# Projection order of a batch's prologue, and written step orders for its attention groups

## The chip, the cores and the metric

One core of one Trainium2 chip runs the whole kernel in one launch. The metric is device time in microseconds (us). The kernel before took 3039.46 us, the median of three runs (3035.17 to 3039.74).

The core's engines are TensorE (PE: matrix products; PEld: its weight loads), VectorE (DVE), ScalarE (ACT), GpSimd (POOL) and SyncE (SP), whose queue starts all DMA transfers here. Each runs its own instruction stream in order; they wait for each other on semaphores.

## The reference, cut to what matters

Two transformer layers on x of shape (2, 1024, 1024), float32. The change concerns the attention of both:

```python
x = x + _L0_attn_ref(_layernorm(x), wq, wk, wv, wo)      # 32 heads of 32, 8 key/value heads
x = x + _L0_ffn_ref(_layernorm(x), ...)                   # mixing of four streams
x = x + _L1_attn_ref(_layernorm(x), Wq, Wk, Wv, Wo)       # the same shape, other rotation
x = x + _L1_ffn_ref(_layernorm(x), ...)                   # gated experts
# attention, per batch entry and head:
q, k, v = x @ wq, x @ wk, x @ wv          # q and k are rotated
scores = q k^T / sqrt(32), causal mask
out = softmax(scores) v;  out @ wo
```

## The kernel before, in words

`attention` (one call per layer, prefix `a_` in the trace) works through two batch entries of 1024 rows. Heads come in eight groups of four, which share one key/value head. A batch has these stages:

- **Prologue.** Six projections of 128 columns each, a *p* in the code, in two halves *c* of 512 rows: keys, keys, queries of group 0, values, values, queries of group 1. Each half is eight pieces of three products (high and low parts of a split float32). VectorE takes a half out of PSUM and rotates it (lines 686, 687), GpSimd finishes the rotation (462, 464), ScalarE and GpSimd split it in two parts (590, 470), SP stores it to DRAM (335, 342) and loads it back stacked in the layout of the scores (352 keys, 345 queries). Values are transposed (953). From the fifth projection on, the row scores of group 0 are interleaved: a *row-score step* S is one bank of query x key products (839), whose maximum VectorE takes (698, 701). 38 such steps give the row maxima of a group; MT transposes them (848), and SP carries them by DRAM into the queries' last row (358, 360).
- **Groups 0 to 5**, the steady ones, as a loop over pairs, three passes. A group's own work is 12 units ST:e.h (four heads, one product each, 886, with ScalarE's exponential, 605, and GpSimd's mask on the diagonal, 494), the products with the values V (902) and with ones D (915), sums of two units on GpSimd (509) and the normalisation of two query halves, NORM (VectorE 746 to 752, behind ScalarE's copies 612 and 618). Interleaved are the row scores S of the next group and the queries' projection P of the group after the next.
- **Group 6** has no projection, **group 7** no row scores. In the first batch group 7 also brings in the next batch's rows: load XL (399), statistics XS (661), scale XN (670), transpose XT (830), evacuation and split XC (584, 677), and the first half of the next batch's first projection.

In every stage the order of instructions is that of a list of steps. For the steady groups it is the text `ORDER`, parsed once; groups 6 and 7 take the same list with what they lack left out, and the next batch's steps are put into it by rules (`iteration`). `bank_plan` gives each S, P, MT and VT step a PSUM bank: in the prologue two of them for S and four for projections, in the groups three for both. In the prologue S follows every piece of 19 (`S_STEPS`), two at a time.

## Time and profile before

| | us |
|---|---|
| median of three runs | 3039.46 |
| the profiled execution's own time | 3036.84 |
| its span in the trace | 3035.1 |
| prologue, batch 0 and 1 of the first layer | 98.0, 91.9 |
| first group, the same | 61.6, 59.5 |
| a steady group | 46.7 |
| last group, batch 0 and 1 | 68.3, 35.4 |

A stage is cut at the first ST product of a group. The trace gives for each instruction its start from the span's beginning, its length and the idle time of its engine before it. Products on PE overlap, so their lengths sum to more than the time; the distance of two starts is what one costs. PEclk is the granted clock of TensorE, 1.00 at full speed.

### The profile page before, as it was taken

What the parts mean: (1) busy time and instruction counts of PE and PEld (TensorE: products, weight loads), DVE (VectorE), ACT (ScalarE), POOL (GpSimd) and SP (SyncE); (2) the same over time, 40 slices, a digit from 0 to 9 for tenths busy, and PEclk for the clock granted to TensorE, in tenths of its full rate; (3) what the DMA queues carried; (4) which work ended last, traced back from release to release, by engine and by line L of the source; (5) the groups of instructions that cost most, each with busy time, mean ns of one, the idle gap of its engine ahead of it and who ended that gap; (6) DMA issues with size and microseconds to landing.
All of it is one profiled execution on the core that took longest, in us unless ns stands there. A gap on an engine that the chain in (4) does not pass through costs nothing. (4 is left out here: it accounts for less than half of the span.)

```text
span 3035.1 us, 50649 instructions
## 1 busy us (share of the span) xinstructions
PE 2620.5 (86%) x15056; PEld 1810.9 (60%) x15056; DVE 1819.1 (60%) x4485; ACT 1081.8 (36%) x2317; POOL 1123.2 (37%) x801
## 2 busy tenths in 40 slices
PE   7799997889998799653768999988799996996999
PEld 6556653655654588542645555545556553885887
DVE  5577775547776433688764666764577774225453
ACT  2155454135555211352511445552155454002000
POOL 7265653445664100000043555636265552001111
PEclk9999998999999899766979999989899998998999
DMA  4223221323231421000233323222323223433111
GB/s 149 87 81 104 64 75 63 117 71 104 77 86 42 161 69 55 0 0 7 83 132 95 106 61 93 73 83 74 90 81 103 64 75 112 146 131 146 63 69 42
DMA packets 121079, 252.95 MB, mean 83 GB/s; under 512 B 12720, under 2 KB 39728, under 8 KB 120880
## 3 DMA queue, kind: packets, MB, share of 16 engines
q1 hardware_dynamic: 120912, 251.03, 25.9%
q8 instruction: 67, 1.10, 0.2%
q14 instruction: 100, 0.82, 0.1%
HBM read 166.57 MB, written 84.41 MB: 83 GB/s over the span
## 5 line engine op out<-in xcount | busy, mean ns | idle before, releaser
L605 ACT ACTIVATE a_prob<-a_pst 128x512 f32<-128x512 f32 (+3 forms) x1536 | 660.7, 493 | 581.8 <-PE a_pst L886 576.2
L698 DVE CUSTOM_DVE_ANT_0 a_psh<-a_psh,a_edge 128x128 f32<-128x128 f32 (+3 forms) x1024 | 479.5, 518 | 247.7 <-PE a_psh L839 218.8
L839 PE MATMUL a_psh<-a_kst,a_qst 127*128 127x512 f32 (+3 forms) x1536 | 494.6, 371 | 79.4 <-DMA a_qst<-q 52.7
L886 PE MATMUL a_pst<-a_qst,a_kst 128*128 128x512 f32 (+2 forms) x1536 | 490.1, 374 | 22.7 <-DMA a_qst<-rowmax 17.8
L509 POOL TENSOR_TENSOR a_prob<-a_prob 128x2048 f32<-128x2048 f32 (+1 forms) x96 | 405.6, 4226 | 241.6 <-PE a_ppv L902 241.6
L839 PEld LDWEIGHTS a_psh<-a_kst,a_qst 127*128 127x128 f32 x1536 | 272.1, 191 | 321.9 <-DVE a_mx L701 104.7
L701 DVE TENSOR_REDUCE a_mx<-a_psh 128x1 f32<-128x512 f32 x512 | 328.2, 685 | 117.3 <-PE a_psh L839 116.4
L886 PEld LDWEIGHTS a_pst<-a_qst,a_kst 128*128 128x128 f32 x1536 | 289.4, 195 | 164.2 <-ACT a_prob L605 105.0
L902 PE MATMUL a_ppv<-a_prob,a_vg 128*32 128x512 f32 (+3 forms) x3072 | 319.8, 503 | 0.0
L915 PE MATMUL a_pden<-a_prob,a_ones 128*32 128x512 f32 (+3 forms) x2304 | 220.4, 475 | 13.8 <-POOL a_prob L509 13.8
L494 POOL TENSOR_SCALAR_AFFINE_SELECT a_prob<-a_prob 128x512 f32<-128x512 f32 x256 | 162.4, 640 | 184.7 <-ACT a_prob L605 184.3
L818 PE MATMUL a_psh<-a_xT_hi,a_w_hi 128*128 128x512 f32 x512 | 210.7, 412 | 16.3 <-DVE a_swp L687 8.5
L818 PE MATMUL a_psh<-a_xT_hi,a_w_lo 128*128 128x512 f32 x512 | 205.1, 401 | 0.0
L818 PE MATMUL a_psh<-a_xT_lo,a_w_hi 128*128 128x512 f32 x512 | 204.8, 400 | 0.0
L462 POOL TENSOR_TENSOR a_swp<-a_swp,a_sin 128x512 f32<-128x512 f32 x80 | 103.4, 1293 | 269.4 <-DVE a_swp L687 258.2
L1480 PE MATMUL h_pout<-h_w,h_o 128*128 128x512 f32 x720 | 167.7, 392 | 0.3 <-DVE h_x L1357 0.3
L1480 PEld LDWEIGHTS h_pout<-h_w,h_o 128*128 128x128 f32 x720 | 134.0, 188 | 28.3 <-issue 0.7
L455 POOL TENSOR_TENSOR a_w_lo<-a_wraw,a_w_hi 128x1024 fp32r<-128x1024 f32 x50 | 119.0, 2381 | 74.4 <-ACT a_w_hi L578 59.5
L698 DVE DVE_READ_ACCUMULATOR2_ANT a_mx<- 128x1 f32 x1024 | 144.3, 141 | 2.9 <-issue 2.9
L902 PEld LDWEIGHTS a_ppv<-a_prob,a_vg 128*32 128x32 f32 x3072 | 70.2, 109 | 104.3 <-issue 64.8
L915 PEld LDWEIGHTS a_pden<-a_prob,a_ones 128*32 128x32 f32 x2304 | 64.4, 111 | 99.5 <-issue 69.8
L1563 PE MATMUL h_pout<-h_w,h_dg 128*128 x256 | 67.1, 408 | 62.9 <-ACT h_dg L1329 44.9
(228 smaller groups left out, 4222.5 us busy)
## 6 DMA issues: line engine op xcount, KB each, us to landing
a_qst<-q SPq DMA_DIRECT2D x192, 256.0 KB, 4.4
a_wraw<-in_wqkv SPq DMA_DIRECT2D x52, 512.0 KB, 4.3
q<-a_stg_hi SPq DMA_DIRECT2D x64, 256.0 KB, 2.1
q<-a_stg_lo SPq DMA_DIRECT2D x64, 256.0 KB, 2.4
a_kst<-kT SPq DMA_DIRECT2D x96, 128.0 KB, 2.6
oT<-a_oT SPq DMA_DIRECT2D x32, 256.0 KB, 2.4
oT<-a_vT SPq DMA_DIRECT2D x32, 256.0 KB, 2.9
h_oraw<-oT SPq DMA_DIRECT2D x16, 512.0 KB, 4.0
```

The costliest lines, as they stand in the source:

```text
L455: pool.tensor_tensor(w[par][1][:, :, :], wraw[par][:, :, :], w[par][0][:, :, :].bitcast(F32), ALU.subtract).then_inc(s["w_ready"], 1)
L494: pool.affine_select(out=blk, in_=blk, compare_op=ALU.is_ge, fill=0.0, base=0, pattern=[[0, GH], [1, P]], channel_multiplier=-1)\
L509: pool.tensor_tensor(into, into, prob[second % len(prob)][:, :, off:], ALU.add)\
L605: act.activation(prob[k % len(prob)][:, h, off:], pst[:, (k * GH + h) % 3, off:], ACT.Exp, scale=scale).then_inc(s["exp_done"], 1)
L698: part = dve.tensor_tensor_reduce(scores, scores, edge[:, BANK - n:], 1.0, 2 * MASKED, ALU.add, ALU.max, mx_hq[kc][:, h, qt:qt + 1])
L701: part = dve.tensor_reduce(mx_hq[kc][:, heads[0]:heads[0] + m, qt], psh[:, at, 0:m * n].rearrange("p (m n) -> p m n", n=n), AX.X, ALU.max)
L818: mm = pe.matmul(bank(at), w[par][a][:, k, :], xT[x][:, k, c * BANK:(c + 1) * BANK], start=(i == 0), stop=(i == len(passes) - 1))
L839: mm = pe.matmul(psh[:, at, i * n:(i + 1) * n], qst[par][0:P - 1, h, qt * P:(qt + 1) * P], kst[par][0:P - 1, kc * BANK:kc * BANK + n], sta ...
L886: pe.matmul(pst[:, (k * GH + h) % 3, off:], kst[par][:, ki * P:(ki + 1) * P], qst[par][:, h, qc * BANK + off:(qc + 1) * BANK], start=True, ...
L902: mm = pe.matmul(ppv[h * HD:(h + 1) * HD, off:], vg[par][:, ki, :], prob[k % len(prob)][:, h, off:], start=(ki == 0), stop=(ki == 4 * qc + ...
L915: mm = pe.matmul(pden[h * HD:(h + 1) * HD, off:], ones[:, :], prob[k[0] % len(prob)][:, h, off:], start=(ki == 0), stop=(UNITS[k[-1]][1] = ...
L1480: mm = pe.matmul(pout[:, half, :], o[:, par, a, k, :], w[:, b, k, half * BANK:(half + 1) * BANK], start=(i == 0), stop=(i == len(passes) - 1))
```

## The change

The prologue's projections come as keys, queries of group 0, keys, values, queries of group 1, values; weights, SP's queue and the waits on stored parts are rearranged to fit. Row scores begin with the fourth projection, one step behind most pieces, 44 pieces in all, over three banks; projections have the other three. The row maxima's transposed copy gets a buffer of its own. The steady order is rewritten; group 6 and group 7 have written orders of their own, and group 7 of the last batch takes its order without the X and P steps.

```diff
@@ the written orders @@
 ORDER = """
-    P:0.0 P:0.1
-    ST:0.0 WL ST:0.1 ST:0.2 S P:0.2 ST:0.3 P:0.3
...
-    ST:11.0 S ST:11.1 ST:11.2 P:1.0 P:1.1 ST:11.3 S P:1.2 S D:8+9 WS V:10 V:11 RK D:10 D:11 MT P:1.3
-      NORM:0 P:1.4 P:1.5 P:1.6 P:1.7 NORM:1 VG
+    P:0.0 S P:0.1
+    ST:0.0 WL ST:0.1 ST:0.2 S P:0.2 S ST:0.3
...
+    ST:6.0 D:3 V:4 S ST:6.1 S ST:6.2 ST:6.3 NORM:0 V:5 SUM:4+5
...
+    ST:11.0 S ST:11.1 P:1.0 ST:11.2 S ST:11.3 P:1.1 RK S WS P:1.2 S D:8+9 V:10 V:11 D:10 D:11 MT P:1.3 VG
+      P:1.4 P:1.5 NORM:1 P:1.6 P:1.7
 """
+ORDER_6 = """
+    S S S S
+    ST:0.0 ST:0.1 ST:0.2 ST:0.3 HI:1
...
+ORDER_7 = """
+    ST:0.0 ST:0.1 ST:0.2 XL:0 ST:0.3 XL:1
...
+    ST:5.0 ST:5.1 XS:4 XL:5 D:3 XT:2 XN:3 XC:2 ST:5.2 V:4 XN:4 ST:5.3 SUM:4+5
...
+    ST:11.0 ST:11.1 XT:7 XC:7 ST:11.2 ST:11.3 V:9 D:8+9 V:10 D:10 V:11 D:11 P:n.0 NORM:1 P:n.1 P:n.2
+      P:n.3 P:n.4 P:n.5 P:n.6 P:n.7
...
-def iteration(full_s=True, proj=True, ahead=False):
...
+def iterations():
+    body, body6, ahead7 = parsed(ORDER), parsed(ORDER_6), parsed(ORDER_7)
+    body7 = [step for step in ahead7 if step[0][0] not in "XP"]
+    for order in (body6, ahead7):
+        assert [step[1] for step in order if step[0] == "D"] == DENS
+        assert [step[1] for step in order if step[0] == "SUM"] == SUMS
+    return (body, parsed(ORDER)), body6, body7, ahead7
 def prologue():
@@ -172,7 +180,7 @@
     out, k, n = [], 0, 0
     for step in order:
         out.append(step)
-        if step[0] == "P" and (4, 0) <= step[1:3] <= (5, 0):
+        if step[0] == "P" and step[1] >= VALUES[0]:
             n += 1
             while k * S_STEPS < n * len(USES) and k < len(USES):
                 out.append(("S", k))
@@ -183,9 +191,9 @@
     return out[PIECES:]
-S_STEPS = 3 * PIECES - 5
-VALUES = (3, 4)
-LO_ORDER = (0, 1, 2, 5)
+S_STEPS = 6 * PIECES - 4
+VALUES = (3, 5)
+LO_ORDER = (0, 1, 2, 4)
 def bank_plan(order, banks, spare=(), carried=None):
@@ -235,9 +243,8 @@
     ZT0, W0, SH0, R0, E0, V0, D0, AC0, N0, ST0, DMA0 = 4, 2, 1, 4, 3, 2, ND, 1, 1, 2, 16
-    pro, bodies, body6, body7 = prologue(), (iteration(), iteration()), iteration(proj=False), iteration(False, False)
-    ahead7 = iteration(False, False, True)
-    plan_pro, U_PRO, _ = bank_plan(pro, (0, 1), spare=(2, 3, 4, 5))
+    pro, (bodies, body6, body7, ahead7) = prologue(), iterations()
+    plan_pro, U_PRO, _ = bank_plan(pro, (0, 1, 2), spare=(3, 4, 5))
     plan, kept, settled = {}, None, False
     while not settled:
         first = kept
@@ -277,7 +284,7 @@
         vg = [sb(f"vg{i}", [P, ST_, HD]) for i in range(2)]
         prob = [sb(f"prob{i}", [P, GH, BANK]) for i in range(4)]
         mx = sb("mx", [P, 2, GH * ST_])
-        mT = vT[0:GH * ST_, 0:P]
+        mT = sb("mT", [GH * ST_, P])[:, :]
         pvs = sb("pvs", [P, BANK])
         dens = sb("dens", [P, BANK])
         rden = sb("rden", [P, BANK // HD])
@@ -330,7 +337,7 @@
             def store_k(b, p):
-                sp.wait_ge(s["q_lo"], b * RB + 2 * p + 2)
+                sp.wait_ge(s["q_lo"], b * RB + 2 * LO_ORDER.index(2 * p) + 2)
                 for part in range(2):
                     sp.dma_start(kT_d[part, ds(b, 1), p * P:(p + 1) * P, :].rearrange("o p n -> p (o n)"),
                                  stg[part][:, :].bitcast(F32)).then_inc(s["k_out"], 16)
@@ -416,23 +423,31 @@
                 sp.wait_ge(s["zT_ready"], ZT0 + (b + 1) * 2 * ST_)
                 sp.sem_inc(s["sp_turn"], 1)
-                for p in range(2, 8):
-                    load_w(b * N_WCHUNK + p, p, p % 2)
-                    if p in (2, 3):
-                        store_k(b, p - 2)
-                    if p in (4, 7):
-                        g = p // 7
-                        sp.wait_ge(s["k_out"], b * 64 + 64)
+                def keys_and_queries(g):
+                    if g == 0:
+                        sp.wait_ge(s["k_out"], b * 64 + 32)
                         sp.sem_inc(s["sp_turn"], 1)
                         sp.wait_ge(s["st_ready"], ST0 + b * NG * NU * GH)
                         sp.sem_inc(s["sp_turn"], 1)
-                        if g == 1:
-                            row_max(b, 0, 0)
-                        stack_keys(b, g, g)
-                        for c in range(2 - g):
-                            sp.wait_ge(s["q_lo"], b * RB + 4 + 2 * g + c + 1)
-                            stack_queries(b * 2 * NG + g * 2 + c, g, c)
+                    stack_keys(b, g, g)
+                    for c in range(2 - g):
+                        sp.wait_ge(s["q_lo"], b * RB + 2 * LO_ORDER.index((1, 4)[g]) + c + 1)
+                        stack_queries(b * 2 * NG + g * 2 + c, g, c)
+                load_w(b * N_WCHUNK + 2, 2, 0)
+                store_k(b, 0)
+                load_w(b * N_WCHUNK + 3, 3, 1)
+                keys_and_queries(0)
+                load_w(b * N_WCHUNK + 4, 4, 0)
+                store_k(b, 1)
+                load_w(b * N_WCHUNK + 5, 5, 1)
+                load_w(b * N_WCHUNK + 6, 6, 0)
+                keys_and_queries(1)
+                load_w(b * N_WCHUNK + 7, 7, 1)
+                sp.wait_ge(s["k_out"], b * 64 + 64)
+                sp.sem_inc(s["sp_turn"], 1)
+                row_max(b, 0, 0)
                 over_groups(b, sp, group, last)
             batches(sp, batch)
@@ -558,13 +573,17 @@
                             pool.drain().then_inc(s["roped"], 1)
                         else:
                             turn_over(u, c)
-                        if c == 1 and p not in VALUES:
-                            for h in range(2 if p < 5 else 1):
+                        if p in (1, 4) and c == 0:
+                            part_lo(b * RB + 2 * LO_ORDER.index(p), 0)
+                        if c == 1 and p in (0, 1, 2):
+                            for h in range(p % 2, 2):
                                 part_lo(b * RB + 2 * LO_ORDER.index(p) + h, h)
-                    if what == "VT" and p == VALUES[1] and piece == [1]:
-                        pool.wait_ge(s["v_ready"], b * 4 + 4)
-                        copy_v(b, 0, 0)
-                        copy_v(b, 1, 1)
+                    if what == "VT" and piece == [1]:
+                        pool.wait_ge(s["v_ready"], b * 4 + 2 + 2 * VALUES.index(p))
+                        pool.sem_inc(s["pool_turn"], 1)
+                        if p == VALUES[0]:
+                            copy_v(b, 0, 0)
+                            copy_v(b, 1, 1)
                 over_groups(b, pool, group, last)
             batches(pool, batch)
@@ -642,12 +661,12 @@
                     w_hi(b * N_WCHUNK + p + 1, b * 6 + (p + 1) // 2, (p + 1) % 2)
                     if p == 1:
                         act.wait_ge(s["k_out"], b * 64 + 32)
-                    if p == 2:
+                    if p == 4:
                         act.wait_ge(s["k_out"], b * 64 + 64)
-                    if p == 5:
-                        act.wait_ge(stacked[0][0], (b * 4 + 1) * QS)
                     if p not in VALUES:
-                        for c in range(2 if p < 5 else 1):
+                        for c in range(2 if p < 4 else 1):
+                            if p == 2:
+                                act.wait_ge(s["q_out"], (b * 2 * NG + c + 1) * 32)
                             part_hi(b * N_WCHUNK + p, c)
                 over_groups(b, act, group, last)
@@ -788,7 +807,7 @@
                         i, at, _ = plan_pro[step]
                         c = step[2]
                         dve.wait_ge(s["sh_ready"], 1 + b * U_BATCH + i + 1)
-                        dve.tensor_copy(vall[:, 4 * c:4 * c + 4, (p - VALUES[0]) * P:(p - VALUES[0] + 1) * P],
+                        dve.tensor_copy(vall[:, 4 * c:4 * c + 4, VALUES.index(p) * P:(VALUES.index(p) + 1) * P],
                                         bank(at).rearrange("p (k n) -> p k n", n=P)).then_inc(s["sh_free"], 1)
                         dve.drain().then_inc(s["v_ready"], 1)
                     if what == "S":
@@ -1938,7 +1957,7 @@
 def qkv_layout(wk, wv, wq):
-    w = np.concatenate([wk, wq[:, :P], wv, wq[:, P:]], axis=1).reshape(KC, P, N_WCHUNK, P).transpose(2, 1, 0, 3)
+    w = np.concatenate([wk[:, :P], wq[:, :P], wk[:, P:], wv[:, :P], wq[:, P:2 * P], wv[:, P:], wq[:, 2 * P:]], axis=1).reshape(KC, P, N_WCHUNK, P).transpose(2, 1, 0, 3)
     return np.concatenate([w, w[:2]], axis=0)
```

SP's queue at the end of the prologue. `a_wraw` are weights, `a_kst` and `a_qst` the stacked keys and queries; before:

```order
L329 DMA a_wraw<-in_wqkv 128x1024 x3
L358 DMA rowmax<-a_vT 32x128
L360 DMA a_qst<-rowmax 1x4096
L352 DMA a_kst<-kT 32x1024 x3
L342 DMA q<-a_stg_hi 128x512
L342 DMA q<-a_stg_lo 128x512
L345 DMA a_qst<-q 32x4x512 x3
```

and now:

```order
L336 DMA a_wraw<-in_wqkv 128x1024 x2
L359 DMA a_kst<-kT 32x1024 x3
L349 DMA q<-a_stg_hi 128x512
L349 DMA q<-a_stg_lo 128x512
L352 DMA a_qst<-q 32x4x512 x3
L336 DMA a_wraw<-in_wqkv 128x1024
L365 DMA rowmax<-a_mT 32x128
L367 DMA a_qst<-rowmax 1x4096
```

The keys and queries of group 1 moved ahead of the last weight load and of the row maxima of group 0.

PE in the first group of the loop, up to the third row-score step (the last row of each; `kst1`, `qst1` are the next group's keys and queries, `w_hi0` and `w_lo0` belong to a projection piece, `a0_pst` takes ST products). Before, seven pieces stand ahead of it, with ten ST products:

```order
L818 MATMUL a0_psh<-a0_xT_hi,a0_w_hi0 128x512
L818 MATMUL a0_psh<-a0_xT_lo,a0_w_hi0 128x512
L818 MATMUL a0_psh<-a0_xT_hi,a0_w_lo0 128x512
L885 ISA
L886 MATMUL a0_pst<-a0_qst0,a0_kst0 128x256
L885 REGISTER_ALU
L886 MATMUL a0_pst<-a0_qst0,a0_kst0 128x256
L818 MATMUL a0_psh<-a0_xT_hi,a0_w_hi0 128x512
L818 MATMUL a0_psh<-a0_xT_lo,a0_w_hi0 128x512
L818 MATMUL a0_psh<-a0_xT_hi,a0_w_lo0 128x512
L837 REGISTER_ALU
L839 MATMUL a0_psh<-a0_kst1,a0_qst1 128x256 x2
```

Now it follows three pieces and three ST products:

```order
L905 MATMUL a0_pst<-a0_qst0,a0_kst0 128x512
L904 REGISTER_ALU
L905 MATMUL a0_pst<-a0_qst0,a0_kst0 128x512
L904 REGISTER_ALU
L905 MATMUL a0_pst<-a0_qst0,a0_kst0 128x512
L856 REGISTER_ALU
L858 MATMUL a0_psh<-a0_kst1,a0_qst1 128x256 x2
L837 MATMUL a0_psh<-a0_xT_hi,a0_w_hi0 128x512
L837 MATMUL a0_psh<-a0_xT_lo,a0_w_hi0 128x512
L837 MATMUL a0_psh<-a0_xT_hi,a0_w_lo0 128x512
L856 REGISTER_ALU
L858 MATMUL a0_psh<-a0_kst1,a0_qst1 128x256 x2
```

The first step moved ahead of the group's second piece, the second and third to either side of its third.

DVE between group 6 and group 7 of a first batch. `a_oT` is the normalised first query half, `a_vT` the second, `a_stg_hi` the next batch's first rows; before:

```order
L707 TENSOR_TENSOR a_mx<-a_mx 128x4x4
L710 COPY a_vT<-a_psh 32x128
L746 STREAM_TRANSPOSE a_oT<-a_dens 128x512
L748 RECIPROCAL a_rden<-a_oT 128x16
L750 STREAM_TRANSPOSE a_dens<-a_rden 128x512
L752 TENSOR_TENSOR a_oT<-a_pvs,a_dens 128x512
L746 STREAM_TRANSPOSE a_vT<-a_dens 128x512
L748 RECIPROCAL a_rden<-a_vT 128x16
L750 STREAM_TRANSPOSE a_dens<-a_rden 128x512
L752 TENSOR_TENSOR a_vT<-a_pvs,a_dens 128x512
L661 BN_STATS a_stat<-a_stg_hi 128x6 x2
L663 BN_AGGR a_mv<-a_stat 128x2
```

and now:

```order
L726 TENSOR_TENSOR a_mx<-a_mx 128x4x4
L729 COPY a_mT<-a_psh 32x128
L765 STREAM_TRANSPOSE a_vT<-a_dens 128x512
L767 RECIPROCAL a_rden<-a_vT 128x16
L769 STREAM_TRANSPOSE a_dens<-a_rden 128x512
L771 TENSOR_TENSOR a_vT<-a_pvs,a_dens 128x512
L680 BN_STATS a_stat<-a_stg_hi 128x6 x2
L682 BN_AGGR a_mv<-a_stat 128x2
```

The first half's four instructions moved up into group 6, behind the products of unit 7.

## Rows read from the trace of the kernel before

**Rows 1.** The page: busy time and share; one group of instructions, mean ns
```profile
PE 2620.5 (86%) x15056; PEld 1810.9 (60%) x15056; DVE 1819.1 (60%) x4485; ACT 1081.8 (36%) x2317; POOL 1123.2 (37%) x801
...
L462 POOL TENSOR_TENSOR a_swp<-a_swp,a_sin 128x512 f32<-128x512 f32 x80 | 103.4, 1293 | 269.4 <-DVE a_swp L687 258.2
```

**Rows 2.** Busy time by stretch, batch 0: length, PE, PEld, DVE, ACT, POOL, clock
```profile
25.40:123.40 98.00, 88.66 (x384) 66.99 (x385) 51.61 (x130) 13.59 (x19) 46.72 (x35) 1.00 0.28 89
123.40:185.00 61.60, 49.33 (x315) 30.71 (x314) 32.30 (x92) 24.80 (x55) 27.18 (x18) 0.89 0.29 81
...
280.10:326.80 46.70, 46.09 (x315) 28.40 (x314) 35.38 (x97) 24.82 (x55) 28.39 (x19) 1.00 0.31 89
...
464.20:532.50 68.30, 51.18 (x305) 26.68 (x305) 36.61 (x63) 29.76 (x67) 24.69 (x19) 0.84 0.20 70
```

**Rows 3.** The same for batch 1: prologue and last group
```profile
532.50:624.40 91.90, 81.11 (x336) 60.27 (x337) 47.52 (x119) 11.30 (x15) 42.67 (x30) 0.97 0.31 101
...
962.70:998.10 35.40, 32.28 (x216) 13.56 (x216) 8.56 (x8) 22.54 (x54) 17.52 (x11) 0.88 0.06 24
```

**Rows 4.** Timeline of PE: start, length, instruction, idle time before it
```profile
40.60 0.39 PE L818 MATMUL a_psh<-a_xT_hi,a_w_hi 128*128 128x512 f32 x1
40.83 0.39 PE L818 MATMUL a_psh<-a_xT_lo,a_w_hi 128*128 128x512 f32 x1
...
135.27 1.11 PE L839 MATMUL a_psh<-a_kst,a_qst 127*128 127x128 f32 x4 [11.02 <-DMA a_qst<-q]
...
137.14 0.63 PE L818 MATMUL a_psh<-a_xT_hi,a_w_lo 128*128 128x512 f32 x1
137.56 0.63 PE L886 MATMUL a_pst<-a_qst,a_kst 128*128 128x512 f32 x1
```

**Rows 5.** Timeline of SP's queue at group 0
```profile
125.55 0.35 SPq L342 DMA_DIRECT2D q<-a_stg_hi  x1
...
128.32 1.28 SPq L345 DMA_DIRECT2D a_qst<-q  x3
```

**Rows 6.** Timeline of PE, prologue of batch 1
```profile
576.02 1.09 PE L953 MATMUL a_psh<-a_ident,a_vT 128*128 128x128 f32 x8 [0.94 <-POOLq L558]
...
611.22 0.28 PE L848 MATMUL a_psh<-a_ident,a_mx 128*32 128x128 f32 x1 [1.28 <-DVE a_mx L707]
```

**Rows 7.** Waits of PE, 532 to 684: total, times, longest
```profile
PE a_pst L818 <- POOL a_w_lo L455: 2.3, 1, 2.3
```

**Rows 8.** Busy time by stretch, row scores of batch 1's prologue
```profile
576.00:611.20 35.20, 29.52 (x121) 18.81 (x121) 29.70 (x87) 2.12 (x2) 5.46 (x4) 1.00 0.30 90
```

**Rows 9.** Timeline of DVE, first maximum after a jump back
```profile
332.76 0.30 DVE L698 CUSTOM_DVE_ANT_0 a_psh<-a_psh,a_edge 128x128 f32<-128x128 f32 x1 [2.26 <-issue]
...
1779.88 0.30 DVE L698 CUSTOM_DVE_ANT_0 a_psh<-a_psh,a_edge 128x128 f32<-128x128 f32 x1 [5.98 <-issue]
```

**Rows 10.** Timeline of SP's queue, a steady group
```profile
385.01 1.28 SPq L345 DMA_DIRECT2D a_qst<-q  x3
```

**Rows 11.** Line 345 from 373 to 420: issue to landing
```profile
DMA to landing us min/median/max: 3.6/4.4/4.9
```

**Rows 12.** Waits in the last group of batch 0
```profile
PE a_psh L830 <- DVE a_xT_lo L677: 7.4, 6, 2.0
...
PE a_pden L915 <- POOL a_prob L509: 4.7, 1, 4.7
```

**Rows 13.** Timelines of four engines, last group of batch 0
```profile
464.24 5.92 PE L886 MATMUL a_pst<-a_qst,a_kst 128*128 128x512 f32 x13 [4.14 <-DMA a_qst<-rowmax]
...
476.62 1.97 PE L830 MATMUL a_psh<-a_ident,a_stg_hi 128*128 128x128 f32 x8 [2.98 <-DVE a_stg_hi L670]
...
467.71 0.36 SPq L399 DMA_DIRECT2D a_stg_hi<-in_x  x1
...
502.55 9.46 POOL L509 TENSOR_TENSOR a_prob<-a_prob 128x2048 f32<-128x2048 f32 x2
...
502.61 4.98 DVE L670 TENSOR_SCALAR a_rots<-a_rots,a_mv 128x1024 f32<-128x1024 f32 x1 [0.66 <-POOL a_mv L450]
```

74 lines of the change are left out of this document (34 added, 40 removed).

## The prediction

> **What bounds the kernel now.** I read the page first. TensorE is busy 86% of the span [rows 1], so a gain is TensorE work removed or a TensorE wait removed; this change removes no product, so only waits count. Then the table by stage, cut at each group's first probability-score product. It shows where the waits are. A steady group (four heads with projections for later ones) takes 46.7 us with 46.1 us of busy TensorE [rows 2]: nothing to win there. Three other stages are slack: the prologue of a batch (98.0 us in batch 0, 91.9 us in batch 1), the first group (61.6 us, three more of the kind at 59.5, 59.4 and 59.7, against 46.7 steady), and the last group of a first batch, which also normalises and transposes the next batch's rows (68.3 us, the second one 67.9, against 35.4 for a last group without that) [rows 2, 3]. The timelines of these stages say what TensorE waits for.
>
> **First group.** TensorE issues three products and then sits 11.02 us until the queries of group 1 are in SBUF [rows 4]. SP's queue shows why: it stores those queries at 125.55 and starts loading them back at 128.32, after the group has begun at 123.4 [rows 5]. They are the prologue's last projection. The wait also costs clock: the granted clock over this group is 0.89, the products behind the wait stand 0.43 us apart instead of 0.23 [rows 4], half speed, until it returns.
> The change projects these queries as the fifth of six, 16 half-steps of a projection (the whole values projection) earlier. A product of 512 columns costs 0.227 us [rows 4], a piece of three 0.68, a projection of 16 pieces 10.9. So the first half of these queries ends 16 + 8 pieces and more than half of the row scores before the group: 16.3 + about 4 + the value transposes, some 21 us. What it needs after that: evacuation, rotation and split (three operations of GpSimd at 1.3 us [rows 1], one of ScalarE and two of VectorE at some 0.7: 6 us, an estimate, 7 with hand-overs), store to load 2.8 [rows 5], loads 1.3 to issue and 4.4 to land [rows 10, 11]: 15.5 us. About 5 us of slack, so the wait goes entirely. What is late next is the row maximum of group 0, whose transpose now stands four pieces before the prologue's end instead of thirteen. In the last group, where nothing covers it, TensorE waits 4.14 us for it [rows 13]; behind the transpose there are now four pieces, two value transposes, their wait and two pieces of group 0, over 7 us. Covered, with 3 us to spare.
> Sum: 61.6 + 59.5 + 59.4 + 59.7 = 240.2 now; four times 47.7 (the steady group and 1 us for what stays) is 190.8. Gain 49. Bounds: 36 (only the waits of 9 us go and the clock stays) and 54.
>
> **Prologue.** From the first value transpose to the row-maximum transpose, 35.2 us [rows 6], all 38 row-score steps are issued, two behind each piece, in two banks. VectorE is busy 29.7 us of these 35.2, TensorE 29.5 [rows 8]: they hand two banks to and fro. TensorE's own work there is 19 pieces x 0.68 = 12.9, row scores of 18,432 columns = 8.2, two pairs of value transposes 2.2, the wait for the maximum 1.3 [rows 6]; 24.6 in all, so 10.6 us are waits on banks. The change spreads the 38 steps over 44 pieces and gives them three banks: about 30 + 8 + 4 = 42 us of TensorE against VectorE's 29.7 plus three more half-evacuations of 0.7 to 1.4 us, 33 us. VectorE has room, so most of the 10.6 goes; I keep 2.6 of it (steps of 0.7 to 1.1 us on VectorE still meet value evacuations) and gain 8 each. Batches 1 and 3 also wait 2.3 us for the second weight chunk [rows 7], since ScalarE's copies behind the last group wait for VectorE's normalisation of the first query half. That normalisation now stands in the last group's tenth unit, so this goes too. Added: one row-score step of group 1 ahead of the group and the value transposes' second wait, now uncovered, together 1 us each. Sum 4 x 8 + 2 x 2.3 - 4 = 33. Bounds: 12 (VectorE keeps the pace) and 42.
>
> **Last group with the next batch's rows.** 68.3 us. Its products, transposes and projection would take 35.4 [rows 3] + 8 x 1.1 + 5.4 = 49.6. The 18.7 between are waits: TensorE for the next rows' first transpose until 476.62 (2.98 us), 7.4 us in six waits for VectorE's evacuation, 4.7 us for one sum of GpSimd [rows 12, 13], and half clock behind them. Three things change. The four row loads start when the group before has stored its second half (467.71 [rows 13]); with the normalisation of the first half moved into that group's unit 7, only one remains in front, some 3 us. The sum of units 4 and 5 moves from behind the seventh rstd to unit 5's end, so the 4.7 goes. The order interleaves one tile per unit; I take half of the 7.4. 3 + 4.7 + 3.7 = 11.4, 11 with rounding, twice: 22. Bounds: 0 and 34.
> VectorE's scale of one tile took 4.98 us while GpSimd's two sums ran for 9.46 us from 502.55 [rows 13], where the others take 0.8. The Trainium skill ("SBUF — State Buffer", Who interferes with whom) says that a VectorE operation in a 2-port mode and a GpSimd operation share one port pair as an exclusive lock, the loser blocked for the whole instruction; the trace agrees. By that rule three scales could still meet a sum in the new order and the last group would keep up to 5 us more; my half of 7.4 leaves room for that.
>
> **Steady groups and the last but one.** 20 and 4 of them. PE's sequence has one run fewer of the 32-column products, below half a us. The first normalisation moves from the end to unit 6: VectorE work beside TensorE's, SP's store of it now ahead of the queries of group g+2, which are not needed before the next group. Two edits take slack away. The third row-score step needs a bank that VectorE has freed; it stands behind three projection pieces instead of seven, 2.7 us and seven products earlier. In exchange 3 us of normalisation no longer stand in front of VectorE's first maximum. And the twelfth step, which needs the second half of the next queries, is reached two products and one run earlier, about 2 us, while their load, started at 385.01 and landing 4.4 us after its issue [rows 10, 11], comes about 1.5 us earlier as the split goes ahead of a mask. I take the whole at 0; bounds a gain of 7 and a loss of 40 (2 us in 20 groups).
>
> **Sum.** Against the profiled execution's own 3036.8 us (its span 3035.1): 49 + 33 + 22 + 0 = 104, 2932.8. The median shown is 2.6 us above the profiled one, so I say 2934.
>
> **Rivals.** *Only the first group gains.* VectorE and GpSimd keep the pace of prologue and last group: for it, VectorE's 84% busy share in the prologue [rows 8]; against it, the ping-pong in two banks. Prologue 12, last group 4: 3036.8 - 49 - 16 = 2972. Chance 0.13.
> *The twelfth step's queries come late.* 2 us in each of 20 groups: 2933 + 40 = 2973, with part of it 2950 to 2973. For it: the load landed only just before in the trace, at 385.86 + 4.4, 15.7 us into a group whose first product stood at 374.6. Against it: the split moves too. Chance 0.12.
> *VectorE's restart, slower side.* At a jump back of the loop over pairs of groups VectorE's first maximum came 2.26 us late in one batch and 5.98 in another with nothing shown that it waited for [rows 9]. The third row-score step is now near enough to the group's start to wait for all of that. The price is up to 5 us, and a wait of that length took the clock down in the first group [rows 4]: some 6 us a group. With three jumps a batch that is 12 x 2 = 24 us, 2957; to end slower than before it must come in every steady group, as it would if VectorE were late at each group's start: 24 x 6 = 144, 3077. It decides from 4.4 us per group on. Chance of that 0.04, against it the odd groups, where the gap in front of the maximum is not there.
> The Trainium skill ("Runtime: NRT & Kernel Launch", Instruction fetch mechanics) says that a taken branch breaks the sequential prefetch and stalls the engine until the target page is fetched. The 2.26 and 5.98 us fit that, and by it the stalls stay at the jumps alone.
> *The change does nothing*: the queries still come last through another wait in SP's queue (the keys of group 1 behind two weight loads). 3030 to 3040, chance 0.02.
>
> **How the numbers follow.** Forecast 0.69, the two partial cases 0.25, slower 0.04, nothing 0.02. What a measurement can tell from no change is about 0.2%, 6 us. Range: the upper end takes in both partial cases, 2976; the lower end takes the better bounds of prologue and last group in part, 9 + 12 + 5: 2906. Faster 0.94, same 0.02, slower 0.04.
>
> **What would show it.** In the changed profile: the first group at 47 to 48 us with a granted clock near 1 and no wait of TensorE on the queries above 1 us; the prologue of batch 1 near 83 us and TensorE's waits in it below 6 us; the last group near 57 us, its SP loads some 3 us sooner after the group before, no wait of 4 us on a GpSimd sum; steady groups at 46 to 48 us. I am wrong if a steady group is over 49 us with a wait in front of its third or twelfth row-score step, or if the prologue stays above 88 us.

## The result and the profile after

The changed kernel takes 2961.52 us (median of 4 runs, 2957.76 to 2964.8) against 3039.6 us for the kernel before in the same session: ratio 0.9741, 95% interval 0.9724 to 0.9759. The forecast was 2934 with a range of 2906 to 2976, so the time lies inside and the sign is right, but 104 us were forecast and 78 came. The profiled execution took 2960.55 us, its span 2958.8.

The page, busy time; the same row stands in [rows 1]:

```profile
PE 2602.2 (88%) x15056; PEld 1805.9 (61%) x15056; DVE 1827.1 (62%) x4485; ACT 1091.0 (37%) x2317; POOL 1114.3 (38%) x801
```

The number of products is the same, as it must be. Busy time by stretch of the changed kernel, columns as in [rows 2, 3]: batch 0's prologue, first group, third group, last but one, last group; batch 1's prologue and the last group without the next batch's rows.

```profile
25.30:117.60 92.30, 85.99 (x388) 70.09 (x389) 53.61 (x138) 13.82 (x19) 48.99 (x36) 0.99 0.37 115
117.60:165.20 47.60, 46.63 (x314) 28.38 (x313) 34.23 (x93) 25.32 (x55) 25.43 (x17) 0.99 0.27 76
212.30:262.30 50.00, 47.93 (x315) 29.27 (x314) 35.14 (x99) 25.20 (x55) 28.01 (x20) 0.97 0.28 83
407.10:455.10 48.00, 40.20 (x257) 20.15 (x256) 32.75 (x81) 23.24 (x53) 20.71 (x14) 0.89 0.12 34
455.10:501.50 46.40, 41.03 (x281) 20.59 (x282) 37.93 (x60) 29.39 (x67) 24.62 (x19) 0.89 0.30 103
501.50:586.80 85.30, 79.71 (x363) 64.70 (x362) 45.79 (x121) 11.12 (x15) 44.32 (x31) 1.00 0.42 127
926.00:963.10 37.10, 32.53 (x216) 12.95 (x216) 6.17 (x4) 21.27 (x51) 17.45 (x11) 0.91 0.04 15
```

Against [rows 2, 3] the first group falls from 61.6 to 47.6 and its clock rises from 0.89 to 0.99; the last group with rows falls from 68.3 to 46.4. But the third group, which took 47.7, takes 50.0, and the last but one, which took 43.6 at a clock of 0.98, takes 48.0 with a clock of 0.89.

One thing about the cut, which is made at each group's first probability-score product and at the last denominator product of a batch: the last group counts 281 products where it counted 305. The 24 that are missing are the next batch's first projection half, which the new order issues behind the last denominators, so they count to the prologue of batches 1 and 3 (363 products against 336). At 0.227 us each they are 5.4 us. With them put back to the last group, all four batches of the two traces sum up so (us; a table worked out from the two traces, not a row of a view):

```
stage (how many)                before   after  change  with the 24 moved  forecast
prologues (4)                    381.5   354.8   -26.7       -37.5            -33
first groups (4)                 240.2   193.8   -46.4       -46.4            -49
steady groups (20)               955.4   978.2   +22.8       +22.8              0
last but one (4)                 174.8   189.9   +15.1       +15.1              0
last with next rows (2)          134.6    92.4   -42.2       -31.4            -22
last without (2)                  68.9    73.6    +4.7        +4.7              0
the rest of the span                -       -     -3.6        -3.6              0
sum (spans 3035.1 and 2958.8)                    -76.3       -76.3           -104
```

So the three stages that were to gain gained 115, more than forecast. The shortfall is 43 us that three stages lost where the forecast said 0. The experiments take up both.

The cut moves a second, smaller piece of work. The new order of the last but one group opens with four row-score steps ahead of its first probability-score product, so they count to group 5, the last steady one: 1920 columns, 0.85 us at 0.227 us for 512, against 0.23 for its own first step, which now counts to group 4. Of the steady groups' 22.8 us some 2.5 therefore only changed sides, and the last but one groups lost about 18.5 and not 15.1.

How the gain looks in the first group. SP's queue and PE in the timeline, batch 0 (start, length, instruction, idle before):

```profile
95.79 0.34 SPq L349 DMA_DIRECT2D q<-a_stg_hi  x1
...
98.55 1.28 SPq L352 DMA_DIRECT2D a_qst<-q  x3
```

```profile
132.70 0.72 PE L858 MATMUL a_psh<-a_kst,a_qst 127*128 127x512 f32 x2 [0.71 <-DMA a_qst<-q]
```

The queries that were stored at 125.55 [rows 5], after the group had begun at 123.4, are stored at 95.79, 22 us before it begins. The wait of 11.02 us [rows 4] is gone; what is left in this group is 0.71 us in front of its twelfth row-score step. In the other three batches' first groups it is 1.5, 0.9 and 2.7 us.

How the loss looks. DVE and PE behind a jump of the loop, at the third group of batch 0. Before, where the group begins at 232.4:

```profile
238.27 0.30 DVE L698 CUSTOM_DVE_ANT_0 a_psh<-a_psh,a_edge 128x128 f32<-128x128 f32 x1 [2.14 <-issue]
```

```profile
239.43 0.50 PE L839 MATMUL a_psh<-a_kst,a_qst 127*128 127x256 f32 x2 [0.87 <-DVE a_mx L698]
```

and now, where it begins at 212.3:

```profile
214.78 0.30 DVE L717 CUSTOM_DVE_ANT_0 a_psh<-a_psh,a_edge 128x128 f32<-128x128 f32 x1 [2.62 <-issue]
```

```profile
215.94 0.50 PE L858 MATMUL a_psh<-a_kst,a_qst 127*128 127x256 f32 x2 [1.81 <-DVE a_mx L717]
```

VectorE idles 2.62 us with nothing shown that it waited for, as in [rows 9]. Its first maximum comes 2.5 us into the group, where it came 5.9 us in: the normalisation in front of it is gone. But TensorE reaches its third row-score step 1.8 us into the group, where without its wait it reached it at 6.2. The step moved by 4.3 us and VectorE by 3.4, so the wait grew from 0.87 to 1.81 us. And in the last but one group of batch 0, three timelines (POOL, DVE, PE):

```profile
430.64 4.55 POOL L524 TENSOR_TENSOR a_prob<-a_prob 128x2048 f32<-128x2048 f32 x1 [0.25 <-PE a_ppv L921]
```

```profile
431.54 4.20 DVE L771 TENSOR_TENSOR a_oT<-a_pvs,a_dens 128x512 f32<-128x512 f32 x1
```

```profile
436.39 0.69 PE L858 MATMUL a_psh<-a_kst,a_qst 127*128 127x384 f32 x1 [3.05 <-DVE a_mx L720]
```

The normalisation's multiply of 128x512 takes 4.20 us instead of 0.69. It starts 0.9 us into GpSimd's sum of a pair of probability units and ends 0.5 us behind it. VectorE's maxima come late by that, TensorE waits 3.05 us, and the clock of the stretch is 0.89. All four groups of this kind show 4.20 or 4.21. The trace of before has the same meeting in the last group of batch 1 (and of batch 3):

```profile
979.15 4.58 POOL L509 TENSOR_TENSOR a_prob<-a_prob 128x2048 f32<-128x2048 f32 x1 [5.63 <-PE a_ppv L902]
```

```profile
979.76 4.51 DVE L752 TENSOR_TENSOR a_oT<-a_pvs,a_dens 128x512 f32<-128x512 f32 x1
```

In the changed kernel the steady groups have it too, in small: their multiply now starts 3.6 to 3.8 us into a sum and takes 1.3 to 1.5 us.

### The profile page after: what moved, and what is told of

Its sections match the earlier page's. It is cut to its first block and busy times, and to the rows that moved or that the text cites. A ratio compares the mean times of both kernels' runs of the same rounds, so it can differ in the third digit from the quotient of the medians.

```text
span 2958.8 us, 50657 instructions
## 1 busy us (share of the span) xinstructions
PE 2602.2 (88%) x15056; PEld 1805.9 (61%) x15056; DVE 1827.1 (62%) x4485; ACT 1091.0 (37%) x2317; POOL 1114.3 (38%) x801
## 5 line engine op out<-in xcount | busy, mean ns | idle before, releaser
L624 ACT ACTIVATE a_prob<-a_pst 128x512 f32<-128x512 f32 (+3 forms) x1536 | 671.3, 492 | 696.6 <-PE a_pst L905 687.5
L858 PE MATMUL a_psh<-a_kst,a_qst 127*128 127x512 f32 (+3 forms) x1536 | 474.0, 364 | 65.3 <-DVE a_mx L717 28.6
L934 PE MATMUL a_pden<-a_prob,a_ones 128*32 128x512 f32 (+3 forms) x2304 | 228.2, 477 | 8.3 <-POOL a_prob L524 7.7
L837 PE MATMUL a_psh<-a_xT_hi,a_w_hi 128*128 128x512 f32 x416 | 172.8, 415 | 8.1 <-DVE a_vall L810 6.5
L837 PE MATMUL a_psh<-a_xT_hi,a_w_lo 128*128 128x512 f32 x416 | 167.0, 402 | 0.0
L837 PE MATMUL a_psh<-a_xT_lo,a_w_hi 128*128 128x512 f32 x416 | 167.0, 401 | 0.0
L921 PEld LDWEIGHTS a_ppv<-a_prob,a_vg 128*32 128x32 f32 x3072 | 79.7, 110 | 122.9 <-issue 73.1
L837 PE MATMUL a_pst<-a_xT_hi,a_w_hi 128*128 128x512 f32 x352 | 139.6, 397 | 6.2 <-DVE a_swp L787 3.2
L837 PE MATMUL a_pst<-a_xT_lo,a_w_hi 128*128 128x512 f32 x352 | 137.8, 392 | 0.0
L837 PE MATMUL a_pst<-a_xT_hi,a_w_lo 128*128 128x512 f32 x352 | 137.6, 391 | 0.0
```

The costliest lines, as they stand in the source:

```text
L624: act.activation(prob[k % len(prob)][:, h, off:], pst[:, (k * GH + h) % 3, off:], ACT.Exp, scale=scale).then_inc(s["exp_done"], 1)
L837: mm = pe.matmul(bank(at), w[par][a][:, k, :], xT[x][:, k, c * BANK:(c + 1) * BANK], start=(i == 0), stop=(i == len(passes) - 1))
L858: mm = pe.matmul(psh[:, at, i * n:(i + 1) * n], qst[par][0:P - 1, h, qt * P:(qt + 1) * P], kst[par][0:P - 1, kc * BANK:kc * BANK + n], sta ...
L921: mm = pe.matmul(ppv[h * HD:(h + 1) * HD, off:], vg[par][:, ki, :], prob[k % len(prob)][:, h, off:], start=(ki == 0), stop=(ki == 4 * qc + ...
L934: mm = pe.matmul(pden[h * HD:(h + 1) * HD, off:], ones[:, :], prob[k[0] % len(prob)][:, h, off:], start=(ki == 0), stop=(UNITS[k[-1]][1] = ...
```

## The experiments

Times are medians; ratios are to the kernel before, run in the same session (3035.0, 3033.3 and 3036.2 us in the three sessions), with a 95% interval.

**The prologue alone.** The three orders of the loop are those of before, with the same step sequences that the kernel before derived.

```
 ORDER = the order of before
 ORDER_6 = "ST:0.0 ST:0.1 ST:0.2 S ST:0.3 ... MT NORM:0 NORM:1"
 ORDER_7 = "XL:0 XL:1 XL:2 XL:3 ST:0.0 ... D:11 NORM:0 NORM:1"
```

> The changed kernel with the three orders of the loop (steady, last but one, last group) put back to those of before: only the prologue's new sequence, its third bank and its queue order stay. Stage sums of the two traces put the net gain of 76 us at prologues -27.5 and first groups -46.4, and the written orders at +22.8 (steady) +15.1 (last but one) -37.4 (last), which is about nothing. Theory A (the parts add up, the prologue carries it): 2962 to 2967 us, first groups at 47 to 48 us. Rival B (the first group needs the new order too, because its queries are used at other steps; with the old order it waits as before): first groups back near 60 us, prologues -27, last groups 0: about 3010 us. Rival C (the last group's shorter time comes from the new prologue, whose weights and first pieces it issues, and not from its order): last groups stay near 47 us beside the next batch's rows, steady groups back at 46 to 47.5: about 2920 us.

2950.44 us (2943.74 to 2956.08), ratio 0.9716 (0.9703 to 0.973). This is 11 us less than the time of the whole change in the medians and 8 by the ratios. Busy time by stretch, the first group of batch 0 and the prologue of batch 1:

```profile
115.80:162.40 46.60, 46.04 (x314) 28.34 (x313) 32.28 (x92) 24.82 (x55) 25.04 (x16) 1.00 0.24 68
509.40:592.20 82.80, 76.58 (x335) 62.01 (x336) 48.28 (x119) 11.42 (x15) 44.36 (x31) 0.97 0.42 134
```

The first group is at full clock and 46.6 us, and does not need the new order: rival B is out. The last groups with rows stand at 68.1 and 67.4, so rival C is out too; theirs is a matter of their order. Theory A had the structure right and was 12 to 17 us too high: the prologues gained 34.8 (the 24 products are in the last group here), and first groups 52.7.

**The orders alone.** The kernel before, with the three written orders.

```
+ORDER_6 = """ ... """
+ORDER_7 = """ ... """
-    pro, bodies, body6, body7 = prologue(), (iteration(), iteration()), ...
+    pro, (bodies, body6, body7, ahead7) = prologue(), iterations()
-        mT = vT[0:GH * ST_, 0:P]
+        mT = sb("mT", [GH * ST_, P])[:, :]
```

> The kernel before with the three written orders alone; its prologue, banks, queue order and chunk order stay. Theory A (parts add up): +23 (steady) +15 (last but one) -37 (last) on 3040 us: 3035 to 3045 us, first groups still near 60 us with the wait of 11 us for the queries. Rival B (the orders are needed for the first group's gain): first groups at 50 us or less, about 3000 us. Rival C (the last group's time comes from the new prologue): last groups stay at 67 us, steady and last but one dearer: about 3078 us.

3050.69 us (3042.26 to 3057.69), ratio 1.0051 (1.0036 to 1.0065): half a per cent slower, and 6 us above theory A. By stages, the steady groups cost 21.1, the last but one 11.9, the last with rows gained 43.1, which is what the parts add up to; but prologues and first groups together cost 21.8 more. The waits of PE in batch 1 from 524 to 650 us show why (total, times, longest):

```profile
PE a_psh L846 <- DMA a_qst<-q: 13.6, 2, 12.7
```

The new steady order has its first row-score step ahead of the group's first product, where the old prologue's late queries are not there. 10.8 of the 21.8 are only the 24 products that change stage. Theory A expected this wait in the first groups, at 60 us; it now falls ahead of the cut, so the first groups read 49 us and the prologues 112. Rival B's 49 us are there, but not its gain: the wait has only changed sides. Rival C is out, the last groups with rows being short on the old prologue too. So the written orders by themselves are a loss here, and the whole gain of the change, and more, is the prologue's.

**The steady order put back.** The changed kernel with `ORDER` alone as before.

```
-    P:0.0 S P:0.1
-    ST:0.0 WL ST:0.1 ST:0.2 S P:0.2 S ST:0.3
+    P:0.0 P:0.1
+    ST:0.0 WL ST:0.1 ST:0.2 S P:0.2 ST:0.3 P:0.3
...
```

> The changed kernel with the steady order alone put back to that of before; the last but one, the last group and the prologue stay as changed. Theory A (the new steady order costs 1 us a group by itself: 20 steady groups +22.8 us by the traces, the first groups unchanged): about 2940 us, the steady groups back at 46 to 47.8. Rival B (the steady groups are longer because of what the new prologue and stores leave them, the banks' parity or the clock): steady groups stay at 47 to 50, 2960 us. Rival C (the last but one group depends on the steady order before it, its first four row-score steps wait on what the last steady group left): that group gets longer still, gain under 15 us.

2946.73 us (2945.96 to 2953.06), ratio 0.9716 (0.9704 to 0.9729): 15 us gained in the medians and 8 by the ratios, whose intervals just overlap; not the 20 of theory A. And it is not gained where theory A put it. The first groups, which run the same order, give 7.2 and the prologues 4.2; the steady groups stay as they were in sum, 978.7. Most of the first four of a batch are back near the times of before, but the fifth, group 5, takes 51.8 to 52.1 us in all four batches (48.2 to 48.9 in the changed kernel, 45.7 to 46.0 before). DVE and PE at its end:

```profile
401.83 1.11 DVE L771 TENSOR_TENSOR a_vT<-a_pvs,a_dens 128x512 f32<-128x512 f32 x1
```

```profile
404.01 0.69 PE L858 MATMUL a_psh<-a_kst,a_qst 127*128 127x384 f32 x1 [3.91 <-DVE a_mx L717]
```

The new last-but-one order opens with four row-score steps in a row. Behind the old steady order VectorE still has both normalisations to do there, and TensorE waits 3.91 us for the maxima. That is rival C in its mechanism: the wait at the seam of two orders takes back what the steady groups gained. The cut counts it to group 5; the last but one itself did not get longer (188.2 in sum against 189.9), as the rival had it. An order has a price only together with the one that runs ahead of it.

**The third row-score step later.** Steps three to five of the steady order one place later; nothing else.

```
-    ST:0.0 WL ST:0.1 ST:0.2 S P:0.2 S ST:0.3
-    ST:1.0 P:0.3 S ST:1.1 P:0.4 HI:1 S P:0.5 ST:1.2 LO:1 ST:1.3
+    ST:0.0 WL ST:0.1 ST:0.2 S P:0.2 ST:0.3
+    ST:1.0 P:0.3 S ST:1.1 P:0.4 HI:1 S P:0.5 ST:1.2 LO:1 S ST:1.3
```

> The changed kernel with one row-score step of the steady order placed later: the third (S:2) leaves its place ahead of ST:0.3, and one step comes in between LO:1 and ST:1.3, so that the third to the fifth step stand one place later each. In the trace TensorE waits 1.98 us there for VectorE's maxima in the groups that follow the loop jump (1.03 before), where VectorE's first maximum stands behind 2.62 us of idle time. Theory A (the steady order costs time because its third step comes before VectorE is back from the jump): the wait below 0.5 us, the 8 groups behind a jump 1 to 2 us shorter: 8 to 16 us, 2946 to 2954 us. Rival B (the steps after it wait instead, VectorE being behind by the same work): within 3 us of 2961.5. Rival C (bunched third to fifth steps run into late maxima): slower, 2966 us or more.

2940.46 us (2939.94 to 2941.87), ratio 0.9692 (0.9676 to 0.9709): 21 us in the medians, 15 by the ratios, more than theory A's range by the one and inside it by the other. The same place as above, DVE, PE and the group's busy time:

```profile
213.24 0.30 DVE L717 CUSTOM_DVE_ANT_0 a_psh<-a_psh,a_edge 128x128 f32<-128x128 f32 x1 [2.62 <-issue]
```

```profile
214.40 0.50 PE L858 MATMUL a_psh<-a_kst,a_qst 127*128 127x256 f32 x2 [0.70 <-DVE a_mx L717]
```

```profile
211.60:259.80 48.20, 46.62 (x316) 28.00 (x315) 35.79 (x104) 25.26 (x56) 28.06 (x20) 1.00 0.30 86
```

VectorE's idle 2.62 us is still there to the hundredth, so the jump's cost is not touched; what changed is that TensorE reaches the step later and waits 0.70 instead of 1.81. The group falls from 50.0 to 48.2 and its clock returns to 1.00. The sum of the steady groups falls from 978.2 to 961.9: 16.3 of their 22.8. In the first batch of the second layer, where the restart is longer, groups fell from 53.3 and 54.0 to 51.4 and 52.0. By the group's number in its batch (us, sums over the four batches, worked out from the three traces):

```
steady groups                       before   after  this run
1 and 3 (8)                          375.6   378.8     376.3
2 and 4, behind a jump (8)           396.1   405.8     391.9
5, ahead of the last but one (4)     183.7   193.7     193.6
```

The move gave 13.9 of its 16 us behind the jumps, more than the 9.7 lost there. Group 5 lost 10.0 and this run does not give them back. Rivals B and C are out. The Trainium skill ("Runtime: NRT & Kernel Launch", Instruction fetch mechanics) ties such a stall to a taken branch whose target is not yet loaded; an idle time that stays while the steps around it move agrees with that. No run here took the jump away, so what the idle time is made of is not shown.

**The normalisation moved, twice.** In the last but one order, NORM:0 stands at the end of unit 7. First it went to unit 6, then to unit 9.

```
first:   ST:6.0 ST:6.1 NORM:0 S S V:4 S ST:6.2 ...
second:  ST:9.0 V:7 NORM:0 ST:9.1 S ST:9.2 ...
```

> The changed kernel with one step of the last but one group moved: the first normalization (NORM:0) goes from the end of unit 7, behind the sum SUM:6+7, to behind ST:6.1, ahead of V:4. In the trace its first VectorE multiply takes 4.2 to 4.5 us in all four such groups, beside GpSimd's sum of 128x2048, against 0.69 to 1.5 elsewhere, and TensorE then waits 3 us for VectorE's row maxima and runs 8 us at half clock. Theory A (VectorE and GpSimd exclude each other in their memory port; the multiply beside the sum is the price of this group): multiply at 0.7 to 1.5 us, wait of 3 us gone, group 47.5 to 43.5 to 44.5: 4 x 3.5 to 4.5 = 14 to 18 us, about 2945 us. Rival B (the group is longer because of its row-score steps in threes and fours, which outrun VectorE's maxima wherever NORM:0 stands): the wait moves and stays near 3 us, 2958 to 2962 us. Rival C (the multiply meets the sum SUM:4+5 instead): 2960 us or above.

2964.61 us (2959.73 to 2965.38), ratio 0.976 (0.9747 to 0.9772): nothing gained, rather 3 us lost in the medians and 6 by the ratios. POOL and DVE:

```profile
424.74 4.50 POOL L524 TENSOR_TENSOR a_prob<-a_prob 128x2048 f32<-128x2048 f32 x1 [8.53 <-PE a_ppv L921]
```

```profile
425.96 3.83 DVE L771 TENSOR_TENSOR a_oT<-a_pvs,a_dens 128x512 f32<-128x512 f32 x1
```

The multiply met the other sum, that of units 4 and 5: rival C. It started 1.2 us into it, took 3.83 and again ended 0.55 behind it. Both multiplies, begun at different depths into a sum, end at the same distance behind it; an exclusion does that, and a mere slowing would not.

> The changed kernel with NORM:0 of the last but one group behind ST:9.0 and V:7, where the changed kernel's trace shows no GpSimd sum from 436.3 to 444.2 us. At ST:6.1 (the run before) its multiply met the other sum: it took 3.83 us, from 425.96 to 429.79, with the sum at 424.74 to 429.24. Theory A (the multiply ends only when GpSimd's sum of 128x2048 ends; away from a sum it takes 0.7 to 1.5 us, and TensorE's wait of 3 us for row maxima goes): the group 47.5 to 44 to 45, about 2948 us. Rival B (row-score steps outrun the maxima in any case): multiply short, the wait for maxima stays above 2 us somewhere in units 6 to 10, 2957 to 2963 us. Rival C (moved to a place where it makes a dense stretch later, third sum of 128x1536 at 444): 2960 us or more with the multiply at 3 us.

2941.34 us (2937.54 to 2946.45), ratio 0.9697 (0.9679 to 0.9716): 20 us in the medians, 13 by the ratios; the last but one groups fall from 189.9 to 172.7 in sum, below the 174.8 of before. POOL, DVE, and the group's busy time:

```profile
429.07 4.59 POOL L524 TENSOR_TENSOR a_prob<-a_prob 128x2048 f32<-128x2048 f32 x1 [0.26 <-PE a_ppv L921]
436.61 3.47 POOL L524 TENSOR_TENSOR a_prob<-a_prob 128x1536 f32<-128x1536 f32 x1 [1.02 <-PE a_ppv L921]
```

```profile
435.28 0.86 DVE L771 TENSOR_TENSOR a_oT<-a_pvs,a_dens 128x512 f32<-128x512 f32 x1
```

```profile
405.40:448.60 43.20, 37.57 (x258) 19.18 (x256) 29.00 (x81) 23.01 (x53) 20.31 (x14) 0.94 0.13 38
```

Between two sums, beside a short mask operation of GpSimd, the multiply takes 0.86, the 3 us wait for maxima is gone, and VectorE is busy 3.75 us less, while the group is 4.8 shorter. The Trainium skill ("SBUF — State Buffer", Who interferes with whom) says that a VectorE instruction with two SBUF inputs contends with a GpSimd instruction that reads SBUF, for a port pair that is locked and not shared. The multiply has two inputs in SBUF, and its three places agree with that.

**The third bank alone.** The kernel before, one line.

```
-    plan_pro, U_PRO, _ = bank_plan(pro, (0, 1), spare=(2, 3, 4, 5))
+    plan_pro, U_PRO, _ = bank_plan(pro, (0, 1, 2), spare=(3, 4, 5))
```

> The kernel before with one line changed: in the prologue the transposes, row-score steps and value transposes use three banks of their group and the projections three spare ones, instead of two and four. Theory A (the third bank does nothing without the spread, because the dense row-score steps are held by VectorE's maxima, and the order of the projections by its evacuation): 3033 to 3040 us. Rival B (two banks held the prologue of before): prologues 3 to 8 us shorter each, 3005 to 3025 us. Rival C (three instead of four banks for the projections hold TensorE at evacuation): slower than 3045 us.

3020.75 us (3017.09 to 3023.44), ratio 0.9954 (0.9938 to 0.997): rival B. The prologues fall from 381.5 to 367.5, 3.5 us each, first groups stay at 60. Theory A is wrong: the bank helps without the spread. The line also takes one of four banks from the projections, so 3.5 us is what both together give.

**The row-score steps dense again.** The changed kernel, three banks kept.

```
-        if step[0] == "P" and step[1] >= VALUES[0]:
+        if step[0] == "P" and step[1:3] >= (4, 1):
-S_STEPS = 6 * PIECES - 4
+S_STEPS = 3 * PIECES - 5
```

> The changed kernel with the prologue's row-score steps in 19 projection pieces of the last 24 again, as dense as before, instead of 44 of the last 48. Three banks stay. On the kernel before the third bank alone gave 12.5 us (prologues 381.5 to 367.5 in sum), the whole new prologue 27 to 35. Theory A (the rest of the prologue's gain is the spread: the maxima of a dense stretch hold TensorE): prologues 3 to 6 us longer each, 12 to 24 us: 2974 to 2986 us, with waits for VectorE's maxima in the last third. Rival B (the sequence did the rest, and the spread nothing): 2958 to 2965 us. Rival C (the dense steps end late and the row maxima of the first group with them, at half clock): first groups above 50 us too, above 2990 us.

2990.57 us (2988.27 to 3000.36), ratio 0.9858 (0.984 to 0.9876): the spread is worth 29 us (36 by the ratios), more than theory A gave. The dense steps stand eight pieces later here than in the kernel before; the 29 us hold for this place and this sequence. The prologues are 384.1 in sum against 354.8; the first groups do not change (193.3), so rival C is out. Timeline of PE in batch 1's prologue, and that stage's busy time:

```profile
556.67 1.09 PE L972 MATMUL a_psh<-a_ident,a_vT 128*128 128x128 f32 x8 [2.38 <-POOLq L573]
...
575.74 0.50 PE L858 MATMUL a_psh<-a_kst,a_qst 127*128 127x512 f32 x1 [0.96 <-DVE a_mx L720]
...
591.00 0.28 PE L867 MATMUL a_psh<-a_ident,a_mx 128*32 128x128 f32 x1 [1.73 <-DVE a_mx L726]
```

```profile
508.70:600.30 91.60, 81.79 (x368) 64.05 (x365) 43.47 (x121) 11.48 (x15) 44.22 (x31) 1.00 0.37 119
```

Against 85.3 us the stage is 6.3 longer. The waits listed for this stage are some 4 us more in sum: in front of the value transposes 3.3 (1.7 in the changed kernel), of the dense steps 1.4 (0), of the maxima's transpose 1.7 (0.6). The other 2.1 us are busy time of TensorE, 81.8 against 79.7 at the same clock; what makes them was not found.

**Queries last.** The changed kernel with the second values ahead of the second queries, as before.

```
-VALUES = (3, 5)
-LO_ORDER = (0, 1, 2, 4)
+VALUES = (3, 4)
+LO_ORDER = (0, 1, 2, 5)
-    w = ... [wk[:, :P], wq[:, :P], wk[:, P:], wv[:, :P], wq[:, P:2 * P], wv[:, P:], wq[:, 2 * P:]]
+    w = ... [wk[:, :P], wq[:, :P], wk[:, P:], wv, wq[:, P:]]
```

> The changed kernel with the prologue's chunks in the sequence keys, queries, keys, values, values, queries: the second queries go from the fifth place to the sixth, the second values from the sixth to the fifth; the third bank, the spread row-score steps, SP's queue and the loop's orders stay. Theory A (the first group's 46 us come from these queries, whose projection ends one chunk earlier; in the kernel before they left the core 2 us after the group's start and TensorE waited 11.0 us for them and ran at half clock): they leave at about 115 us, the queue delivers them some 5 to 8 us behind that, the first groups' twelfth step needs them 10 to 15 us into the group: the wait is back with 4 to 12 us, the first groups at 54 to 60 us, in all 2985 to 3010 us, prologues as in the changed kernel. Rival B (the spread steps and the queue did it, since the rope work of the last chunk is no longer behind dense maxima): first groups at 47 to 50 us, 2958 to 2968 us. Rival C (with queries last the prologue's own end waits too): prologues above 88 us as well, above 3015 us.

3001.93 us (2991.89 to 3003.76), ratio 0.9888 (0.9873 to 0.9904): 40 us lost, 45 by the ratios. The profiled execution is the fastest of them, 31 us above that of the changed kernel; by its stages the prologues cost 30.5 and the first groups 6.1. SP's queue and PE just ahead of batch 1's first group, which begins at 602.6:

```profile
590.01 0.34 SPq L349 DMA_DIRECT2D q<-a_stg_hi  x1
...
592.78 1.28 SPq L352 DMA_DIRECT2D a_qst<-q  x3
```

```profile
598.96 1.11 PE L858 MATMUL a_psh<-a_kst,a_qst 127*128 127x128 f32 x4 [5.05 <-DMA a_qst<-q]
```

The wait for the queries is back, 5.05 us in this batch. Theory A has the mechanism and the total, and missed the place: the written steady order puts the first row-score step ahead of the group's first product, so the wait falls to the prologue's side of the cut, as rival C had it for another reason. Sequence 40, spread 29 and bank 12.5 make 82, near the 85 that the new prologue gave alone. That is no check of the parts: the first two were measured by taking them out of the changed kernel, the third by adding it to the kernel before.

**The last group's order alone, on the new prologue.** Old steady and last but one order; the new last order only where the next batch's rows are beside it.

```
 ORDER, ORDER_6 = the orders of before
 ORDER_7 = the new one
-    body7 = [step for step in ahead7 if step[0][0] not in "XP"]
+    body7 = [step for step in parsed(ORDER_7_END) if step[0][0] not in "XP"]
```

> The changed kernel's prologue, with the steady and the last but one order of before, and of the new orders only the last group's, used where the next batch's rows are read beside it (the last batch's own last group as before). The prologue alone gave 2950.4 us, and its last groups beside the next rows stood at 68.3 and 67.7 us, against 46.1 and 46.9 with the new order, while the prologues behind them were 82.8 against 85.3. Theory A (parts add up: 2 x (21.7 - 2.4) = 39 us off 2950): 2909 to 2914 us, steady groups 46 to 48, last but one 43.5, last with rows 46 to 47. Rival B (the new last group is only short because the last but one group before it is long and leaves row maxima and loads ready): last groups 52 us or more, above 2925 us. Rival C (the prologue after it gives the time back): prologues of batches 1 and 3 at 90 us or more, 2925 us or more.

2918.69 us (2917.84 to 2920.92), ratio 0.9622 (0.9606 to 0.9639): the fastest version, 43 us under the changed kernel, and 5 short of theory A. The last groups are 50.2, not 46. SP and PE:

```profile
440.03 0.36 SPq L387 DMA_DIRECT2D oT<-a_oT  x1
443.82 0.36 SPq L387 DMA_DIRECT2D oT<-a_vT  x1
444.30 0.36 SPq L421 DMA_DIRECT2D a_stg_hi<-in_x  x1
```

```profile
452.63 1.97 PE L864 MATMUL a_psh<-a_ident,a_stg_hi 128*128 128x128 f32 x8 [3.76 <-DVE a_stg_hi L704]
```

The next batch's first row tile is asked for 3.8 us into the group (it begins at 440.5), behind two stores of the output in SP's queue. The second store waits until the second normalisation, the last step of the group before, is done; its multiply ran from 443.10. In the changed kernel the tile is asked for at the group's start, and this wait does not exist:

```profile
454.40 0.36 SPq L372 DMA_DIRECT2D oT<-a_vT  x1
454.89 0.36 SPq L406 DMA_DIRECT2D a_stg_hi<-in_x  x1
```

**The same with the normalisation earlier.** One move in that version's last but one order.

```
-    ST:6.0 S S ST:6.1 ...                 ... D:11 MT NORM:0 NORM:1
+    ST:6.0 NORM:0 S S ST:6.1 ...          ... D:11 MT NORM:1
```

> The version with the new prologue, the old steady and last but one order and the new last group (2918.7 us), and one step moved: NORM:0 of the last but one group from its end to behind ST:6.0, where no GpSimd sum runs (406.7 to 415.7 us in that version's trace) and VectorE has idle time. In that version the first four row tiles of the next batch are asked for at 444.30 us, 3.8 us into the last group, because the SP queue issues the output's two stores first, and TensorE waits 3.8 us for the first tile's VectorE work; in the changed kernel they are asked for at 454.89, at the group's start, and this wait is not there. Theory A (the loads are late through the queue, so the earlier NORM:0 gives the last group its 4 us): last groups with rows at 46 to 47 instead of 50.2, 2909 to 2913 us. Rival B (the second store, of NORM:1, holds the queue anyway): the loads still 3 us into the group, 2915 to 2920 us. Rival C (NORM:0 in unit 6 delays VectorE's maxima): last but one group 2 us longer each, 2918 us or above.

2926.91 us (2922.11 to 2930.74), ratio 0.964 (0.9625 to 0.9655). Theory A and rival C both held and the second won: the last groups with rows fell from 100.4 to 91.5 in sum (the load is asked for at 445.94, the group begins at 446.2), and the four last but one groups rose from 174.5 to 191.7. Rival B is out, as the load no longer comes into the group. POOL, DVE and PE:

```profile
416.48 4.58 POOL L539 TENSOR_TENSOR a_prob<-a_prob 128x2048 f32<-128x2048 f32 x1 [8.49 <-PE a_ppv L936]
```

```profile
419.54 2.06 DVE L786 TENSOR_TENSOR a_oT<-a_pvs,a_dens 128x512 f32<-128x512 f32 x1
```

```profile
422.67 0.50 PE L873 MATMUL a_psh<-a_kst,a_qst 127*128 127x512 f32 x1 [2.80 <-DVE a_mx L732]
```

The step was put into a gap of GpSimd that ended at about 415.7, but VectorE runs it in order behind the maxima of the steps ahead, and came to the multiply at 419.54. It met the sum and ended 0.54 us behind its end, for the third time.

**Both mended.** The changed kernel with the third row-score step later and NORM:0 in unit 9.

> The changed kernel with both single moves together: the third row-score step of the steady order later (alone 16.3 us in the steady groups' sum) and NORM:0 of the last but one group away from GpSimd's sum (alone 17.2 us in that group's sum). Theory A (two separate causes, which add up): ratio to before 0.9741 - 0.0054 - 0.0055 to 0.963, 2922 to 2930 us; the written orders then cost the steady groups 6 us and gain 2 in the last but one and 42 in the last. Rival B (one cause, VectorE being short of time, so that the second move finds nothing left): 2936 to 2942 us.

2922.75 us (2918.35 to 2930.07), ratio 0.9631 (0.9614 to 0.9649). Busy time by stretch, the third group and the last but one of batch 0:

```profile
209.80:257.80 48.00, 46.65 (x314) 27.98 (x314) 35.02 (x99) 25.23 (x55) 28.02 (x19) 1.00 0.29 86
401.00:443.80 42.80, 37.58 (x258) 19.21 (x256) 29.00 (x81) 23.03 (x53) 20.31 (x14) 0.94 0.13 39
```

The two causes add up: steady groups 961.1 in sum (961.9 with the one move alone), last but one 171.7 (172.7 with the other alone). Rival B is out. Two moves in a table of words give back 39 us (33 by the ratios), and with them the changed kernel is level with the best version above: 0.9631 and 0.9622 have overlapping intervals.

## Why the prediction came out as it did

**The number.** The sum of the parts, 2932.8, with the 2.6 us between profiled execution and median is 2935; I wrote 2934. The measured time lies inside the range, but by luck in part: I had set the upper end for two cases, a prologue and last group that gain little and a twelfth step that waits everywhere. Neither came at its price. What came was a loss in stages that I had taken at 0, and one of my signs of being wrong was met: the steady groups behind a jump take 49.1 to 54.0 us, with a wait of 1.7 to 4.7 us in front of the third row-score step.

**The first group: right.** 49 forecast, 46.4 measured; 47.6, 48.1 and 47.4 against the 47.7 forecast, and 50.7 in the last batch, where the twelfth step waits 2.7 us for queries. I had said no such wait above 1 us; two of four are above. Which batch has the long one is not fixed: in the version with the third step later it is batch 1, with 2.4 us, and batch 3 has 0.7. The experiment with the queries last shows that the sequence is the cause.

**The prologue: right in kind, a little low.** 33 forecast, 37.5 measured with the 24 products put back (34.8 in the experiment with the old orders, where nothing has to be put back). I had named two causes, the spread and the bank, and a later step for the second weight chunk. PE's wait for that chunk, 2.3 us [rows 7], is indeed not among those of the changed kernel's prologue of batch 1, where this is all that is over 0.6:

```profile
PE a_psh L972 <- POOLq L573: 1.7, 2, 0.9
PE a_psh L837 <- DVE a_vall L810: 1.6, 1, 1.6
PE a_pst L837 <- DVE a_swp L706: 1.5, 1, 1.5
```

The prologue of batch 1 was forecast at 83 and reads 85.3; without the 5.4 us that the cut adds it would be 80.

**The last group with rows: right in kind, too low.** 22 forecast, 31.4 measured. The waits went nearly as the steps said. Of the 7.4 us for VectorE's evacuation [rows 12] 3.6 remain, the 4.7 for GpSimd's sum is 0.6, the 2.98 for the first tile is gone:

```profile
PE a_pst L905 <- DMA a_qst<-rowmax: 4.1, 1, 4.1
PE a_psh L849 <- DVE a_xT_lo L696: 3.6, 1, 3.6
...
PE a_pden L934 <- POOL a_prob L524: 0.6, 2, 0.4
```

That is 10.9 of waits, against the 11.4 of my sum, and 15.7 were gained. What the sum left out is the clock, as far as the rows show it: the mean granted clock rises from 0.84 to 0.89, which is some 22 us at half speed before and 10 now (an estimate from the two means and lengths). I had priced that for the first group and not for this one. No run separates it from the waits. The 3.6 us that remain are the cost that I had left room for: in the changed kernel one scale of a row tile, at 482.69, again takes 4.93 us, beside a sum of GpSimd from 482.51 to 487.08, and the evacuation that TensorE waits for stands behind it on VectorE. No run moved it. The order itself is the cause: added alone to the new prologue it took the two groups from 135.5 to 100.4, 24 us with the 24 products put back. The earlier loads, which I put at 3 us, are worth 4.3 us beyond that in batch 0 (50.2 to 45.9 in the version with the normalisation earlier).

**Steady groups and last but one: "I take the whole at 0". This step failed,** by 38 us. It had three parts.

- *The third row-score step.* I named the edit, the restart of VectorE [rows 9] and a bound of 40 us, and then took 0 for the forecast. My reason was that 3 us of normalisation no longer stand in front of VectorE's first maximum. They did come off, 3.4 us measured; but my own figures for the step, 2.7 us and seven products earlier, make 4.3 us, which is what the trace shows. I set the one against the other without taking the difference, in places where TensorE already waited 0.87 us. In the six groups behind a jump outside the second layer's first batch TensorE waited 0.81 to 1.01 us before and 1.68 to 2.11 now; the two with the long restart did not get worse (4.7 and 4.9 before, 4.4 and 4.7 now). Moving the step back gave 16.3 us, 13.9 of them behind the jumps. The rival "VectorE's restart" had put the price at 24 us for twelve places behind a jump, of which eight begin a steady group and lost 9.7, so it was the right mechanism at too high a price; I gave it a chance only in its form of every group, which did not come.
- *The seam ahead of the last but one group.* The last steady group of a batch lost 10.0 us in the four batches, and none of my terms spoke of it. Some 2.5 are the row-score steps that the cut moves. The rest is argued from the trace alone: TensorE waits 0.82 to 1.19 us for VectorE's evacuation of a projection in front of those four steps, and 0.5 to 0.8 us on queries at the twelfth. Over all steady groups the waits on queries come to 10.4 us, against 2.6 before, so "the twelfth step's queries come late" can have come at a fifth of its 40 us at most; no run moved that step.
- *The first normalisation in the last but one group.* I treated its move only as what it frees at the group's end, and did not ask what it now stands beside. I had written down what VectorE loses beside GpSimd's sum, 4.98 us for an operation of 0.8 [rows 13], but for the last group's scales alone. The move set the multiply beside a sum in all four groups, 4.20 instead of 0.69 us; taking it away from the sum gave 17.2 us, with the wait and the half clock behind it.

The last groups without rows lost 4.7 us in sum, which no step of mine spoke of; in the fastest version, with the old order in that place, they take 68.7, the 68.9 of before.

In sum, 42.6 us were lost in stages that I had set at 0, 11.3 more than forecast came in the three others, and 3.6 in the rest of the span: 104 - 42.6 + 11.3 + 3.6 = 76.3.

## What to carry to other kernels

When an order of steps is rewritten, price each moved operation twice: for what it leaves, and for what it now stands beside on the other engines; an in-order queue that lags by several us makes its place in time another than its place in the list. If a trace shows an engine restarting late at a loop jump, keep the steps that need it out of the first few us behind the jump. And a wait on TensorE can cost more than its length, since the products behind it may run at half clock: 17.2 us in four groups here for four waits of 3.05 us.

## What the runs showed of the hardware

- A VectorE multiply of 128x512 from two SBUF operands, 0.69 us alone, did not end before GpSimd's running 128x2048 TENSOR_TENSOR: started 0.6, 0.9, 1.2 and 3.1 us into it, it took 4.51, 4.20, 3.83 and 2.06 us and ended each time 0.5 to 0.6 us behind the sum. Started 1.6 us behind one it took 0.86. The sum itself took 4.50 to 4.59 us in all five places. A VectorE scale of 128x1024, 0.80 us alone, took 4.93 beside such a sum and ended 0.5 us behind it.
- VectorE's idle time at the jump of the loop belongs to the place: at the third group of batch 0 it is 2.14 us before, with the normalisation ahead of it, 2.62 in the changed kernel and again 2.62 with the third row-score step moved.
- The mean granted clock of a group was lower where TensorE waited longer: 0.97 in the third group with one wait of 1.81 us in front of a step, 1.00 with 0.70 there; 0.89 in the last but one group with a wait of 3.05, 0.94 without it.
- Three banks instead of two for VectorE's and TensorE's hand-over, with three instead of four left to the projections, gave 3.5 us per prologue even where the steps stayed dense.
